# Two graph-attention layers on one core: column totals taken from the attention product instead of a sum of their own

## The reference, cut to what matters

```python
scores = (Wh @ a1)[:, None] + (We @ a2)[None, :]      # layer 0: We from E, layer 1: from x
e = where(scores > 0, scores, alpha * scores)
e = where(adj > 0, e, very_negative)
attention = softmax(e, axis=1)
out0 = elu(attention @ E + x)                         # layer 0
out1 = attention @ (x @ W1) + bias                    # layer 1
x = layernorm(x + out)
```

## Time and profile before

| what | value |
|---|---|
| median of 3 runs | 678.38 us (677.52 to 679.47) |
| profiled execution, its own time | 681.98 us |
| span of that execution | 680.2 us |
| busy share of the span: DVE, PE, ACT, POOL | 84%, 77%, 76%, 27% |
| adjacency halves loaded | 64 of 1 MB each |

### The profile page before, as it was taken

The page is one execution under the profiler, slowest core; times in us unless marked ns, Lnnn a source line. Parts: engine busy times, 40 slices in busy tenths (PEclk is TensorE's granted clock), DMA queues, the critical chain, the costliest instruction groups (busy, mean ns, idle before and its releaser), DMA issues.

```text
span 680.2 us, 14220 instructions
## 1 busy us (share of the span) xinstructions
PE 523.2 (77%) x6038; PEld 233.3 (34%) x6039; DVE 570.2 (84%) x729; ACT 516.8 (76%) x592; POOL 184.8 (27%) x143
## 2 busy tenths in 40 slices
PE   1304788987988879899998804777898888899894
PEld 1202344433433334443454402223333333333341
DVE  3888998998678886889646889999999999899585
ACT  0846997997978979687966503997998989789673
POOL 0120000475006850284038000001520560131150
PEclk9999978997979889999998965999999989999998
DMA  7899885776565655331200000000000000000000
GB/s 170 325 346 319 279 321 213 249 249 205 199 224 186 219 197 199 125 125 64 70 3 2 18 3 28 2 4 29 1 9 33 1 1 17 16 1 17 1 17 9
DMA packets 18631, 76.46 MB, mean 112 GB/s; under 512 B 6552, under 2 KB 8776, under 8 KB 10376
## 3 DMA queue, kind: packets, MB, share of 16 engines
q1 hardware_dynamic: 17560, 74.63, 32.1%
q0 software_dynamic: 256, 0.80, 0.4%
q10 hardware_dynamic: 752, 0.13, 0.1%
HBM read 74.47 MB, written 1.09 MB: 111 GB/s over the span
## 4 chain that ended last, share of the span: by engine, by line
DVE 20%; PE 15%; ACT 8%; issue 7%; POOL 3%; POOLq 0%; ACTq 0%; DVEq 0%
DVE junk L711 9%; PE acc L930 9%; ACT Pm L602 7%; DVE zps L805 6%; PE zps L975 5%; PE acc L937 1%; DVE tAB L686 1%; DVE tot L746 0%; PE zps L904 0%; POOL rstd L456 0%; POOL tAB L424 0%; POOL tAB L403 0%; POOL tAB L402 0%; POOL X L419 0%; DVE tot L742 0%
## 5 line engine op out<-in xcount | busy, mean ns | idle before, releaser
L602 ACT ACTIVATE Pm<-zps,ebias 128x1024 f32<-128x1024 f32 (+1 forms) x320 | 293.5, 934 | 101.0 <-DVE zps L805 73.7
L711 DVE CUSTOM_DVE_ANT_0 junk<-v,u_row 128x2048 int8<-128x2048 int8 (+3 forms) x136 | 301.8, 2241 | 2.7 <-ACT v L495 2.5
L975 PE MATMUL zps<-D,v 128*128 128x128 bf16 x2048 | 175.9, 226 | 50.1 <-DVE D L733 29.6
L805 DVE SCALAR_TENSOR_TENSOR zps<-S_row,tau_col,zps 128x1024 f32<-128x1024 f32 (+1 forms) x136 | 141.9, 1050 | 67.7 <-PE zps L975 65.3
L975 PEld LDWEIGHTS zps<-D,v 128*128 128x128 fp8e4 x2048 | 120.7, 100 | 211.1 <-issue 87.0
L594 ACT ACTIVATE zps<-S_row,ntau_col 128x1024 f32<-128x1024 f32 (+1 forms) x184 | 176.6, 960 | 5.3
L930 PE MATMUL acc<-Pm,VE 128*32 128x512 f32 (+1 forms) x1280 | 153.0, 552 | 16.5 <-ACT tAB L537 8.4
L930 PE MATMUL acc<-Pm,X 128*32 128x512 f32 (+1 forms) x1280 | 145.2, 526 | 22.4 <-ACT Pm L602 16.2
L387 POOL TENSOR_TENSOR tAB<-flag,totW 128x520 f32<-128x520 f32 (+1 forms) x8 | 10.0, 1246 | 338.7 <-issue 188.2
L937 PE MATMUL acc<-Pm,ones 128*32 128x256 f32 (+1 forms) x1280 | 89.2, 352 | 0.0
L937 PEld LDWEIGHTS acc<-Pm,ones 128*32 128x32 f32 x1280 | 43.6, 116 | 75.9 <-issue 66.4
(11 more groups left out here) (147 smaller groups left out, 281.4 us busy)
## 6 DMA issues: line engine op xcount, KB each, us to landing
adj_in<-in_adj SPq DMA_DIRECT2D x64, 1024.0 KB, 5.1
S_row<-S_rows_scratch SPq DMA_DIRECT2D x5, 512.0 KB, 3.8
S_row<-S_rows_scratch SPq DMA_DIRECT2D x3, 256.0 KB, 3.0
u_row<-u_row_scratch SPq DMA_DIRECT2D x3, 256.0 KB, 4.0
out<-tAB SPq DMA_DIRECT2D x3, 256.0 KB, 2.7
S_row<-S_rows_scratch POOLq DMA_DIRECT2D x1, 512.0 KB, 11.6
S_row<-S_rows_scratch POOLq DMA_DIRECT2D x1, 256.0 KB, 7.9
out<-tAB SPq DMA_DIRECT2D x2, 128.0 KB, 2.0
```

What stands on the lines that cost most here:

```text
L602: a.activation(Pm[:, k % PB, 0:R(C) * P], zps[:, buf("step", k), 0:R(C) * P], ACT.Exp, bias=ebias[:, int(seeded(k)), J:J + 1])\
L711: d.tensor_tensor_reduce(out=junk[:, at % 2, 0:cols.stop - cols.start], in0=v_bytes[:, rt, cols], in1=u_row[:, cols], scale=1.0, scalar=-3 ...
L805: d.scalar_tensor_tensor(z, S_row[:, C % 2, 0:R(C) * P], tau_col[:, J:J + 1], z, ALU.max, ALU.add).then_inc(z_done, 1)
L975: last = t.matmul(zps[:, buf("step", k), r * P:(r + 1) * P], v[:, chunks[C][1] + r, J * P:(J + 1) * P], D[:, C % 2, r, :], start=(r * P % ...
```

## The change

The sum over rows comes out of `product`. A column of ones is kept in all three `Pm` buffers at column 512, just behind the 512 columns of a chunk of 4 tiles. In chunks 0 and 5 the second half (s = 1) of the product reads 257 columns instead of 256, so `acc` column 256, partitions 64 to 127, accumulates the totals of V over all rows. DVE sets the ones for layer 0 right after `t_col` in the setup; POOL sets them again for layer 1, after its epilogue of chunk 3, since chunks 1 to 3 overwrite column 512. `column_totals`, `totals`, two semaphores and the ring's user `totals` are gone.

The rest of the work on the totals moves from the first chunk to the second of each layer: `save_totals` stands at J = 2 of chunks 1 and 6, inside `save_acc` and ahead of its copies, and reads 128 columns spread from `acc`; `totals_W` stands at J = 3 on PE, ahead of that step's products, and `save_totals_W` at J = 4 on ACT, ahead of that step's seeds and exponential. `totals W` thus takes a buffer of `zps` between steps 2 and 3 of the second chunk.

The lists of seeded steps follow from the ring. By the rule of lines 224 to 230, the unseeded steps of chunk 0 go from 0, 1, 4, 7 to 0, 1, 2; of chunk 1 from 0, 1, 2, 6, 24 to 0, 1, 2, 4, 6, 24; of chunk 5 from 0, 1, 4, 7 to 0, 1, 2, 3; of chunk 6 from 0, 1, 2, 3, 5, 6, 9, 12, 15, 18, 20, 23, 26, 29 to 0, 1, 2, 3, 4, 6, 8, 11, 14, 17, 20, 23, 26, 29. The other chunks keep theirs, and 184 steps are seeded in both kernels.

In layer 1 the totals are now those of features 1 to 63 and of the ones (the columns that the product uses), while W1's rows are not shifted. This term is multiplied by the flags, which are all 0 here; the instructions and their shapes are the same either way.

```diff
-        W1d = sb("W1d", [F, F])
+        W1d = sb("W1d", [P, F])
...
-        totrep = tAB[0:F, 0:P]
+        ONES_AT = WIDTHS[0][0] * P
+        totrep = tAB[F:2 * F, CW - P:CW]
...
-                if C in FIRSTS:
-                    users += [("totals", layer(C))] * (J == 2) + [("totals W", layer(C))] * (J == 5)
-                else:
+                if C - 1 in FIRSTS:
+                    users += [("totals W", layer(C))] * (J == 3)
+                if C not in FIRSTS:
                     users += [("sums", C - 1)] * (J == 4) + [("rows", C - 1)] * (J == 22 and layer(C) == 0)
...
+                if C == NC - 2:
+                    pool.wait_ge(pv_done, JT * (C + 1))
+                    g.memset(Pm[:, :, ONES_AT:ONES_AT + 1], 1.0).then_inc(ones_set, 1)
...
             def save_totals(l):
-                act.wait_ge(tot_done, l + 1)
-                a.activation(totrep, zps[0:F, buf("totals", l), 0:1].broadcast_to([F, P]), ACT.Copy)\
+                w = WIDTHS[l][0] // 2 * P
+                a.activation(totrep, acc[F:2 * F, 0, w:w + 1].broadcast_to([F, P]), ACT.Copy)\
                     .then_inc(totrep_saved, 1)
...
+                if C in FIRSTS:
+                    save_totals(layer(C))
                 sums = a.activation(acc_sums[:, 0:w], acc[:, 0, 0:w], ACT.Copy)
...
                         if J == 2:
                             save_acc(C - 1)
+                        if J == 4 and C - 1 in FIRSTS:
+                            save_totals_W(layer(C))
...
-                    elif J == 3:
-                        save_totals(layer(C))
-                    elif J == 6:
-                        save_totals_W(layer(C))
...
+            d.memset(Pm[:, :, ONES_AT:ONES_AT + 1], 1.0).then_inc(ones_set, 1)
...
-                    if J == 1 and C in FIRSTS:
-                        column_totals(layer(C))
...
+                if first and C in FIRSTS:
+                    pe.wait_ge(ones_set, layer(C) + 1)
                 for s in range(2):
+                    cols = w + int(s == 1 and C in FIRSTS)
                     for f in range(0, F, G):
-                        last = t.matmul(acc[s * F + f:s * F + f + G, 0, 0:w], V[:, f:f + G],
-                                        Pm[:, k % PB, s * w:(s + 1) * w], start=first, stop=end)
+                        last = t.matmul(acc[s * F + f:s * F + f + G, 0, 0:cols], V[:, f:f + G],
+                                        Pm[:, k % PB, s * w:s * w + cols], start=first, stop=end)
...
                     if C not in FIRSTS:
+                        if J == 3 and C - 1 in FIRSTS:
+                            totals_W(layer(C))
                         if J == 4:
                             project(C - 1)
...
-                    elif J == 2:
-                        totals(layer(C))
-                    elif J == 5:
-                        totals_W(layer(C))
```

More of the change, by code:

```diff
@@ L130, in build @@
         wabs = tA[:, 2, 0:F]
-        colsum = tA[:, 7, 0:F]
-        totrep = tAB[0:F, 0:P]
+        ONES_AT = WIDTHS[0][0] * P
+        assert all(w[0] == WIDTHS[0][0] and 2 * w[0] <= RT for w in WIDTHS)
+        totrep = tAB[F:2 * F, CW - P:CW]
         zps = ctx.enter_context(nc.psum_tensor("zps", [P, ZB, CW], F32))
@@ L219, in wait_buf @@
                 what, number = users[n - ZB]
-                eng.wait_ge({"step": exp_done, "sums": o_saved, "rows": rows_saved, "totals": totrep_saved,
+                eng.wait_ge({"step": exp_done, "sums": o_saved, "rows": rows_saved,
                              "totals W": totW_saved, "u": u_saved}[what],
@@ L484, in _ @@
             act.wait_ge(memsets, 1)
-            act.dma_start(W1d[:, :], W1).then_inc(W1d_loaded, 16)
+            act.dma_start(W1d[F:2 * F, :], W1).then_inc(W1d_loaded, 16)
             for half in range(2):
@@ L883, in spread_ext @@
                     .then_inc(ext_spread, 1)
-            def totals(l):
-                pe.wait_ge(colsum_done, l + 1)
-                wait_buf(pe, "totals", l)
-                t.matmul(zps[0:F, buf("totals", l), 0:1], colsum, ones[:, 0:1], start=True, stop=True)\
-                    .then_inc(tot_done, 1)
             def totals_W(l):
@@ L893, in totals_W @@
                 wait_buf(pe, "totals W", l)
-                t.matmul(zps[:, buf("totals W", l), 0:F], totrep, (identf[0:F, 0:F], W1d[:, :])[l],
+                t.matmul(zps[:, buf("totals W", l), 0:F], totrep, (identf, W1d)[l][F:2 * F, -F:],
                          start=True, stop=True).then_inc(totW_done, 1)
```

5 lines of the change are left out of this document (1 added, 4 removed).

## The result

The changed kernel took 685.61 us (median of 4 runs, 685.16 to 686.03) beside 678.92 us (4 runs, 677.52 to 681.37) for the kernel before: ratio 1.0089, 95% interval 1.0065 to 1.0113. Forecast were 678.8 us, within 675.5 to 681.2, and no change that can be told. So it is slower, by more than twice the 0.3% bound, and the time lies outside the range.

The account below looks back on a forecast made before the run. No engine was taken to be far ahead (DVE 84%, PE 77%, ACT 76%), so the bound differs by stage. Terms -0.7 + 1.8 - 2.8 + 2.1 = +0.4 us on the median 678.38 gave 678.8 us, range 675.5 to 681.2.

Parts of the forecast that it names:

- Chunk 5, -2.8: Chunk 5: without DVE's sum, step 3's exponential starts at about 420.3, then 1.33 us per step; 2.8 us shorter.
- Chunk 0, -0.7: Chunk 0: step 2 waits behind a transferred half, so ACT's 3.05 us idle stays; 0.7 us shorter.
- Chunk 6, +2.1: Chunk 6: step 4, now unseeded, waits for the copy of totW, delaying ACT's exponentials; 2.1 us longer.
- Chunk 1, +1.8: Chunk 1: moved pieces and unseeded step 4 delay DVE's maxima, with no slack to the chunk's end; 1.8 us longer.
- lower bound of 0.9: Chunk 1: least cost, +0.9 us, if DVE has no idle time: the step alone less 0.32.
- idle 1.0 us: Chunk 1, step 4: DVE, free since 121.3, waits until 122.3 for PE's products, 1.0 us.
- rival (c): PE falls to its low clock in chunk 6: +1.8 us there, +2.2 in all, 680.6 us; chance 0.16.
- (a): Step 4's stall is hidden: chunk 1 costs 0.9, chunk 6 nothing; -2.6 in all, 675.8 us; chance 0.15.
- (b): All work removed in chunks 0 and 5 counts: 7.4 us off, some 0.5 back, 671.5 us; chance 0.05.

Follow-up runs that it names:

- e1: Kernel before without any column totals (no sum, products or copies; totW zeroed once): 677.60 us, ratio 0.9963.
- e2: Changed kernel, but totals W written into the unused half of the projection's buffer, not its own ring user; step 4 seeded as before: 677.99 us, ratio 0.9968.
- e13: Changed kernel, unchanged, one more profiled execution: 676.16 us.
- e15: Changed kernel, unchanged, another profiled execution: 680.97 us.
- e3: Kernel before with its sum and totals product, but totals W and its copy moved to J = 3 and 4 of the second chunks: 682.45 us, ratio 1.0034.
- e12: Changed kernel plus idle PE products at J = 4 of chunk 6 and J = 2 of chunk 1: 680.36 us, ratio 1.0004.
- e6: Kernel before, ring and totals unchanged, with the changed kernel's lists of unseeded steps in chunks 1 and 6: 683.08 us, ratio 1.0040.
- e7: Changed kernel with its ring, but step 4 of chunks 1 and 6 seeded by ACT and the old lists there: 682.73 us, ratio 1.0037.
- e11: Changed kernel in layer 0; in layer 1 totals W goes into the projection's buffer as in e2: 675.72 us, ratio 0.9958.
- e9: Changed kernel once more, unchanged, 12 runs beside the others on one chip: 681.42 us, ratio 1.0029.
- e4: Kernel before once more, unchanged, 10 runs and a second profile: 678.60 us, ratio 0.9992.
- e14: Changed kernel, unchanged, another profiled execution: 684.97 us.
- e10: Changed kernel, but at J = 4 of chunks 1 and 6 DVE does its row maximum ahead of step 4's instruction: 680.04 us, ratio 1.0018.

## Why the prediction was wrong

**Chunk 5, -2.8: right**, in size and by its steps. 420.3 was reckoned for step 3's exponential on the old clock of the span; 421.70 less the 1.43 us by which chunk 5 started later in the changed kernel is 420.27. Pitch 1.33 as read. e1 and e2 give the same 44.34.

**Chunk 0, -0.7: right within its spread** (57.42 after 58.10), with the order as told. DVE waited 0.56 us for the half, and 0.56 to 0.60 in the other four profiles. But the five profiles of the changed kernel lie between 57.20 and 57.79 and the two of before at 57.85 and 58.10, so between the means it is -0.5, and that the first pair gives -0.7 to a tenth is luck.

**Chunk 6, +2.1: the mechanism right, the forecast half of what the profile shows.** The price of the wait itself is 2.32 us: 61.67 (e13), 61.68 (e15, e3) and 61.66 (e12) against 59.35. Its parts: e6 shows that 1.4 us come from the list of unseeded steps even without the ring's user; e7 shows no gain from seeding step 4 again as long as its buffer comes late; e2 that all is gone when user and list go together. How the 2.3 us split between list and late buffer when both are there was not tried further. The other 2.4 us are PE at 1.2 GHz behind the wait (granted 0.66 against 0.91), shown by e13 and e15, the same kernel without them; e12's ten runs fit this.

**Chunk 1, +1.8: near the measured value at a middling clock, with a mechanism that hangs on the clock.** With a clock of 0.86 in its first steps, which the kernel before has too, the changed kernel or its layer 0 gives 79.14, 78.21 and 78.78 (e11), against 77.44 and 76.22: +0.8 to +2.9, about +1.9 between the means (78.71 and 76.83). At 0.72 it is 80.33: another 1.6. At 1.00 it is 77.24 (e13) against 76.83 and 76.82 in e1 and e2, which have no user there and the old list: +0.4, below the forecast's lower bound of 0.9, since DVE then has no idle time at step 4. The idle 1.0 us was worked out from the earlier trace rows, in which PE is at the lower level in the chunk's first steps (a product of 1.89 us), and was taken for the change's own. So the 1.8 is met only where a low stretch is there too.

**The step that failed is rival (c).** The sum prices both second chunks at the clock of the rows and has nothing for a further fall behind the waits that the change adds; the runs have +2.4 us for it in chunk 6 and +1.6 in chunk 1. The text put it as an event in chunk 6 alone, at 1.8 us, with a chance of 0.16, "less than half because the pauses that PE has there now, 0.64 and 0.65 us, leave it at the high level". Its price was near (2.4 measured), its consequences were seen, but it was taken for a property that the kernel either has or has not. The runs show something that differs between executions of one kernel, in more than one place: 8 of the 16 timed runs of the changed kernel had 0.935 and 683.8 us or more. Why all four of the result are among them, and only 4 of the 12 of e9, stays open. The reason given for less than half was also read from too few rows: the earlier trace rows show the later waits of PE, and the kernel before has longer ones in the same chunk, at a clock of 1.00:

```profile
463.64 1.06 PE L930 MATMUL acc<-Pm,X 128*32 128x512 f32 x8 [1.83 <-ACT tAB L532]
...
467.93 0.62 PE L975 MATMUL zps<-D,v 128*128 128x128 bf16 x8 [1.03 <-ACT zps L594]
```

In the changed kernel the first of these is 2.26 us, and in e13 and e15 the low stretch came behind it. And chunk 1, where the earlier trace rows already showed a product of 1.89 us behind a wait of 2.69, was given a price at the clock that it then had, though the change lengthens that very wait. With (c) at one in two and at 4 us over both chunks, the forecast would have been +0.4 or +4.4 by turns, 678.8 or 682.8 us. Over all 16 timed runs of the changed kernel, two sessions taken together, the median is 682.7 us, some 0.4% above the kernel before (679.7 to 680.3 in the sessions); in e9's session alone it is 0.3%. So it is slower, by less than half of what the first four runs said.

In terms of the sum, 6.8 us are missing: 2.6 in chunk 6, 1.1 in chunk 1, less the 0.7 by which the start came out shorter, 0.5 by which the median of before moved from three runs to four, and 3.3 of the base. This last is a reading of its own: the sum was made against a profile at 681.98 us, and its distance of 3.6 us to the median was carried over as a constant. e4 shows that 2.5 us of the distance are low-clock stretches in chunks 1 and 2, of which the profile before had more. Sum by profiles: +3.4 us for after minus before; by medians of the result +6.7; the difference of 3.3 is that the kernel before met fewer of them in its four runs than in its profile, and that the changed kernel was at 0.935 in its profile and in all of its four.

Of the other rivals, (a) had it that the stalls are hidden: no length of chunk 6 supports that, while chunk 1 at a clock of 1.00 does; (b) that 7.4 us count: e1 gives 0.37% (about 2.5 us) as the whole that can be had.

## What to carry to other kernels

An instruction that uses a slot of a ring is paid for by whoever comes one turn later, so put a small product into the unused part of a slot that is taken anyway (e2: the whole cost gone), and look at what a planner derives from the ring, since a moved user also moves its lists (e6: 1.4 us in chunk 6). Price a new wait of TensorE twice, at its length and at the lower clock behind it, and give the second a chance per execution; if several executions of one kernel spread by half a per cent, compare profiles chunk by chunk at like clocks before reading a difference of medians. Taking work off the busiest engine gives only up to the next engine's pitch: 7.4 us removed were worth 2.8 in one stage and 0 to 0.7 in the other, where a transfer stood behind them. And a stage that a change does not touch can differ by more than the change is worth (chunk 2: 81.48 to 85.42 us), so leave such stages out of the comparison.

## What the runs showed of the hardware that was not expected

Pauses of PE of 2.3 to 2.6 us are followed by 1.2 GHz in some executions and not in others. In three profiles of the changed kernel (first, e9, e14: granted 0.66) the low stretch comes in the pause of 2.60 us ahead of step 4 of chunk 6; in e10, where that pause is 2.60 us as well but DVE's order differs, the clock stays at 1.00. In e13 and e15 the low stretch had come earlier, behind the wait of 2.26 us for `acc`: step 1's product took 1.94 us, so the pause ahead of step 4 was only 1.02 and 1.13 us long, and the products behind it took 0.62. What draws the one or the other is not settled: the instructions and their order are the same in these five. Idle products (bf16, 512 columns; 7 recorded in 1.67 us, 11 in 2.54) put into such pauses went with a level of 1.00 in both places in the profile of e12, and its ten runs end at 680.99 us where the changed kernel's go to 685.68. That they are the cause is likely from this and not shown: e10 and e13 have one place each at 1.00 without them.
